# State space loop of a vision tower: the heads' products turned to channels on partitions

## The reference, cut to what matters

```python
z = zxbcdt[..., :D_INNER]                       # D_INNER = 256, the gate
xBC = silu(causal_conv(zxbcdt[..., 256:768], 4 taps) + conv_b)
xs, Bc, Cc = xBC[..., :256], xBC[..., 256:384], xBC[..., 384:]     # xs as 4 heads of 64
h = h * dA_t + (dt_t * x_t) * B_t               # scan over the 36 tokens
y_t = einsum('bhpn,bn->bhp', h, C_t)
y = ys + D_skip * xs
y = y * silu(z)
y = y * rsqrt(mean(y * y, -1) + 1e-05) * gnorm_w
return y @ W_out
```

## Time and profile before

| | |
|---|---|
| median of 3 runs | 1536.03 us (1534.56 to 1537.8) |
| the profiled execution | 1539.4 us |
| its span in the trace | 1537.6 us |
| TensorE matmul busy | 1271.7 us, 83% of the span |
| VectorE busy | 768.6 us, 50% |
| ScalarE busy | 736.6 us, 48% |
| GpSimd busy | 389.9 us, 25% |
| the state space stage | about 490 to 669 us of the span |

### The profile page before, as it was taken

How to read it: one execution, slowest core, us unless ns; L and a number is a source line. 1 busy time by engine, 2 the same in 40 slices (tenths; PEclk the granted TensorE clock), 3 DMA queues, 4 the chain that set the end, 5 groups by cost and what they waited for, 6 DMA issues and landing times. The chain is left out here.

```text
span 1537.6 us, 34523 instructions
## 1 busy us (share of the span) xinstructions
PE 1271.7 (83%) x10636; PEld 1111.1 (72%) x10636; DVE 768.6 (50%) x2481; ACT 736.6 (48%) x2620; POOL 389.9 (25%) x721
## 2 busy tenths in 40 slices
PE   6999579999983899945357599996799889947996
PEld 3777469999972899845357588885799777835885
DVE  0388641111125477734665345555533248863775
ACT  0488434444421455531124167663344248831895
POOL 0156510100001166632347100001101011111452
PEclk9999869999995899968579799998799979976998
DMA  6000010100001000000232100000000100012442
GB/s 235 13 1 0 1 35 15 28 14 14 14 0 42 1 1 0 0 14 1 84 104 49 55 1 0 0 0 1 28 18 17 37 6 1 0 38 65 137 136 66
DMA packets 41923, 48.88 MB, mean 32 GB/s; under 512 B 8085, under 2 KB 31236, under 8 KB 41580
## 3 DMA queue, kind: packets, MB, share of 16 engines
q1 hardware_dynamic: 34876, 36.79, 8.1%
q0 software_dynamic: 4176, 6.56, 1.6%
q10 hardware_dynamic: 2784, 4.47, 0.8%
HBM read 41.78 MB, written 6.56 MB: 31 GB/s over the span
## 5 line engine op out<-in xcount | busy, mean ns | idle before, releaser
L964 ACT ACTIVATE f_hid<-quad_bank,f_b1s 128x512 f32<-128x512 f32 (+1 forms) x240 | 147.9, 645 | 188.0 <-PE quad_bank L895 187.8
L1009 DVE SCALAR_TENSOR_TENSOR f_y<-bank,GATE,f_y 128x128 f32<-128x128 f32 x288 | 81.0, 344 | 253.7 <-PE bank L908 253.5
L908 PEld LDWEIGHTS bank<-f_w2s,f_hid 128*128 128x128 f32 x1728 | 201.7, 192 | 3.7
L908 PE MATMUL bank<-f_w2s,f_hid 128*128 128x128 f32 x1728 | 203.2, 275 | 0.0
L895 PE MATMUL quad_bank<-f_xp,f_w1p 128*128 128x512 f32 (+1 forms) x720 | 168.4, 383 | 16.8 <-DVE f_xp L990 16.8
L459 ACT ACTIVATE a_E<-quad_bank,a_shift 108x108 f32<-108x108 f32 x528 | 177.6, 356 | 4.3 <-DVE a_shift L523 3.9
L895 PEld LDWEIGHTS quad_bank<-f_xp,f_w1p 128*128 128x128 f32 x720 | 125.6, 193 | 37.8 <-issue 17.0
L459 ACT ACTIVATION_READ_ACCUMULATOR a_E<-quad_bank,a_shift 108x1 f32 x528 | 112.7, 213 | 0.0
L299 POOL TENSOR_TENSOR a_ve<-a_mv,const 108x1 f32<-108x1 f32 x66 | 12.5, 190 | 391.8 <-DVE a_mv L578 391.8
L1551 PE MATMUL bank<-ss_xp,ss_wtap 128*128 128x108 f32 x704 | 88.0, 284 | 23.2 <-DVE ss_xp L1631 20.3
L368 PE MATMUL quad_bank<-a_qk 19*108 19x108 f32 (+1 forms) x1056 | 101.3, 275 | 3.4 <-ACT a_E L459 0.6
(11 more groups left out here) (369 smaller groups left out, 2807.1 us busy)
## 6 DMA issues: line engine op xcount, KB each, us to landing
a_wqk<-in_a_wqk SPq DMA_DIRECT2D x24, 256.0 KB
pats<-in_patches SPq DMA_DIRECT2D x3, 1296.0 KB, 18.7
a_wo<-in_a_wo SPq DMA_DIRECT2D x24, 128.0 KB, 2.0
pats<-in_patches ACTq DMA_DIRECT2D x2, 1296.0 KB, 14.3
f_w1s<-in_f_w SPq DMA_DIRECT2D x8, 256.0 KB, 2.7
f_w2s<-in_f_w SPq DMA_DIRECT2D x8, 256.0 KB, 3.0
f_w1a<-in_f_w SPq DMA_DIRECT2D x1, 2048.0 KB, 9.9
f_w2a<-in_f_w SPq DMA_DIRECT2D x1, 2048.0 KB, 14.6
```

The costliest lines, as they stand in the source:

```text
L908: mm = pe.matmul(m.bank[n % 2][0:W, g * D:(g + 1) * D], hid[:, n % 2, c, g * W:(g + 1) * W], w2s[:, u, c * 128:(c + 1) * 128], start=(c == ...
L964: act.activation(hid[:, n % 2, c, 0:k * W], m.quad_bank[:, (n * chunks + c) % 4, 0:k * W], func, bias=b1s[:, u, c:c + 1]).then_inc(hid_rea ...
L1009: ins = dve.scalar_tensor_tensor(out=h, in0=y[:, (g - c0) * D:(g - c0 + 1) * D], scalar=m.GATE[:, bass.ds(e + g * 8, 1)], in1=h, op0=ALU.m ...
```

## The change

The gate's product is turned: the weights are stationary and the input moves, so z comes out with channels on partitions, as two matmuls of 128 channels by 108 tokens. No copy of the input is needed. The heads' products are turned the same way: each head's dt x is stationary (64 columns), its decay matrix moves, and the result lies at PSUM partitions 0 to 63 or 64 to 127, two heads side by side and two one behind the other. `xd` is made from the silu result, which has channels on partitions already, with D as a column. `ys`, `yz`, `zs` are [128, 216]. yz is then the stationary operand of the output projection as it is: its transposes and the copy `yT` are gone. The sum of squares over channels is now a sum over partitions: ScalarE squares yz, and TensorE multiplies the squares (stationary) with a column of ones, two matmuls that accumulate; ScalarE reads that with scale 1/256 and bias epsilon, and GpSimd makes one instruction of rms, in step t for group t-4, behind n1 of t-5. `xd` stands first in GpSimd's step. The D row is not loaded any more. The core of the diff, declarations left out:

```diff
         def _(pool):
+            pool.wait_ge(w_loaded, 64)
+
             def step(t, par):
                 q = 1 - par
-                if live(t, 1):
-                    g = t - 1
-                    at_least(pool, z_psum, g - 1)
-                    pool.tensor_copy(xTs[:, q, :], m.XT[:, bass.ts(g, P)]).then_inc(xts_ready, 1)
+                if live(t, 2):
+                    g = t - 2
+                    pool.wait_ge(silu, g + 1)
+                    at_least(pool, ys_ready, g - 1)
+                    pool.tensor_tensor(xd[:, par, :, :], sx[:, par, 0:2, :], ch[:, 22:24].unsqueeze(2).broadcast_to([128, 2, P]),
+                                       ALU.mult).then_inc(xd_ready, 1)
                 if live(t, 5):
...
-                if live(t, 3):
-                    g = t - 3
+                if live(t, 4):
+                    g = t - 4
                     pool.wait_ge(ssq_ready, g + 1)
-                    pool.tensor_tensor(ssq[:, q, :], ssq[:, q, :], m.inv_cw[0:P, :], ALU.mult).then_inc(rms_steps, 1)
-                    pool.wait_ge(rms_steps, g * 2 + 1)
-                    pool.tensor_tensor(ssq[:, q, :], ssq[:, q, :], m.eps[0:P, :], ALU.add).then_inc(rms_steps, 1)
-                    pool.wait_ge(rms_steps, g * 2 + 2)
                     at_least(pool, sum_ready, g - 1)
-                    pool.tensor_tensor(rms[:, q, :], ssq[:, q, :], m.mhalf[0:P, :], ALU.pow).then_inc(rms_ready, 1)
+                    pool.tensor_tensor(rms[:, par, :], ssq[:, par, :], m.mhalf[0:P, :], ALU.pow).then_inc(rms_ready, 1)
...
-                    pe.wait_ge(xts_ready, g + 1)
                     at_least(pe, z_ready, g)
-                    pe.matmul(m.bank[1][0:P, 0:CW], xTs[:, par, :], win[:, 0:CW], start=True, stop=True).then_inc(z_psum, 1)
-                if live(t, 4):
-                    g = t - 4
-                    pe.wait_ge(yz_ready, g + 1)
-                    at_least(pe, yt_ready, g)
                     for c in range(2):
-                        mm = pe.transpose(m.bank[0][:, c * P:(c + 1) * P], yz[:, par, c * 128:(c + 1) * 128], m.ident[0:P, 0:P])
-                    mm.then_inc(yt_psum, 1)
+                        mm = pe.matmul(m.bank[1][:, c * P:(c + 1) * P], win[:, c * 128:(c + 1) * 128], m.XT[:, bass.ts(g, P)], start=True, stop=True)
+                    mm.then_inc(z_psum, 1)
...
                     for n in range(NS):
-                        cols = slice(n * 64, (n + 1) * 64)
-                        mm = pe.matmul(y_bank[0:P, cols], M[:, q, n, :], xdt[:, q, cols], start=True, stop=True)
+                        mm = pe.matmul(y_bank[n % 2 * 64:(n % 2 + 1) * 64, n // 2 * P:(n // 2 + 1) * P], xdt[:, q, n * 64:(n + 1) * 64], M[:, q, n, :],
+                                       start=True, stop=True)
                     mm.then_inc(y_psum, 1)
+                if live(t, 4):
+                    g = t - 4
+                    pe.wait_ge(sq_ready, g + 1)
+                    at_least(pe, ssq_ready, g)
+                    for c in range(2):
+                        mm = pe.matmul(m.bank[0][0:P, 0:1], sq[:, par, c * P:(c + 1) * P], m.one, start=(c == 0), stop=(c == 1))
+                    mm.then_inc(ssq_psum, 1)
...
-                    pe.wait_ge(yt_ready, g + 1)
+                    pe.wait_ge(yz_ready, g + 1)
                     at_least(pe, sum_ready, g)
                     for c in range(2):
-                        mm = pe.matmul(o_bank[0:P, 0:D], yT[:, c * P:(c + 1) * P], wout[:, c, :], start=(c == 0), stop=(c == 1))
+                        mm = pe.matmul(o_bank[0:P, 0:D], yz[:, par, c * P:(c + 1) * P], wout[:, c, :], start=(c == 0), stop=(c == 1))
...
-                    act.wait_ge(yt_psum, g + 1)
-                    at_least(act, o_psum, g)
-                    act.activation(yT[:, :], m.bank[0][:, 0:2 * P], ACT.Copy).then_inc(yt_ready, 1)
+                    act.wait_ge(ssq_psum, g + 1)
+                    at_least(act, rms_ready, g - 1)
+                    act.activation(ssq[:, par, :], m.bank[0][0:P, 0:1], ACT.Identity, scale=m.inv_cw[0:P, :], bias=m.eps[0:P, :]).then_inc(ssq_ready, 1)
...
-                    act.activation(sq[:, :], yz[:, q, :], ACT.Square, accum_out=ssq[:, q, :]).then_inc(ssq_ready, 1)
+                    act.activation(sq[:, q, :], yz[:, q, :], ACT.Square).then_inc(sq_ready, 1)
...
                     dve.wait_ge(xd_ready, g + 1)
-                    dve.tensor_tensor(ys[:, :], xd[:, q, :], y_bank[0:P, 0:CW], ALU.add).then_inc(ys_ready, 1)
+                    dve.tensor_tensor(ys[:, :], xd[:, q, :, :].rearrange("p c j -> p (c j)"), y_bank[:, 0:2 * P], ALU.add).then_inc(ys_ready, 1)
```

More of the change, by code:

```diff
@@ L1393, in state_space_phase @@
         silu = sem("silu")
-        xts_ready = sem("xts_ready")
         xc_psum = sem("xc_psum")
@@ L1409, in state_space_phase @@
         yz_ready = sem("yz_ready")
+        sq_ready = sem("sq_ready")
+        ssq_psum = sem("ssq_psum")
         ssq_ready = sem("ssq_ready")
-        rms_steps = sem("rms_steps")
         rms_ready = sem("rms_ready")
-        yt_psum = sem("yt_psum")
-        yt_ready = sem("yt_ready")
         o_psum = sem("o_psum")
@@ L1428, in state_space_phase @@
         wtap = sb("wtap", [128, TAPS, 512])
-        drow = sb("drow", [P, NS])
-        xd = sb("xd", [P, 2, CW])
-        ys = sb("ys", [P, CW])
+        xd = sb("xd", [128, 2, 2, P])
+        ys = sb("ys", [128, 2 * P])
         xp = sb("xp", [128, 2, TB, PADDED])
@@ L1435, in state_space_phase @@
         sx = sb("sx", [128, 2, 4, P])
-        xTs = sb("xTs", [128, 2, P])
         cum = sb("cum", [P, 2, NS, P])
@@ L1442, in state_space_phase @@
         xdt = sb("xdt", [P, 2, CW])
-        zs = sb("zs", [P, 2, CW])
-        yz = sb("yz", [P, 2, CW])
-        sq = sb("sq", [P, CW])
+        zs = sb("zs", [128, 2, 2 * P])
+        yz = sb("yz", [128, 2, 2 * P])
+        sq = sb("sq", [128, 2, 2 * P])
         ssq = sb("ssq", [P, 2, 1])
         rms = sb("rms", [P, 2, 1])
-        yT = sb("yT", [128, 2 * P])
         yt = sb("yt", [P, 2, D])
@@ L1460, in _ @@
         def _(sp):
-            for dst, src in ((win, io["ss_win"]), (ch, io["ss_ch"]), (drow, io["ss_drow"])):
+            for dst, src in ((win, io["ss_win"]), (ch, io["ss_ch"])):
                 sp.dma_start(dst[:, :], src).then_inc(w_loaded, 16)
@@ L1509, in _ @@
         def _(pe):
-            pe.wait_ge(w_loaded, 80)
+            pe.wait_ge(w_loaded, 64)
             pe.wait_ge(prepared, 4)
@@ L1581, in step @@
                     at_least(act, mix_ready, g - 1)
-                    at_least(act, xd_ready, g - 1)
                     act.activation(xc[:, par, :], m.bank[3][0:P, 0:CW + P], ACT.Copy).then_inc(xc_ready, 1)
@@ L1585, in step @@
                     at_least(act, yz_ready, g - 1)
-                    act.activation(zs[:, par, :], m.bank[1][0:P, 0:CW], ACT.Tanh, scale=0.5).then_inc(z_tanh, 1)
+                    act.activation(zs[:, par, :], m.bank[1][:, 0:2 * P], ACT.Tanh, scale=0.5).then_inc(z_tanh, 1)
                 if live(t, 4):
                     g = t - 4
-                    act.wait_ge(yt_psum, g + 1)
-                    at_least(act, o_psum, g)
-                    act.activation(yT[:, :], m.bank[0][:, 0:2 * P], ACT.Copy).then_inc(yt_ready, 1)
+                    act.wait_ge(ssq_psum, g + 1)
+                    at_least(act, rms_ready, g - 1)
+                    act.activation(ssq[:, par, :], m.bank[0][0:P, 0:1], ACT.Identity, scale=m.inv_cw[0:P, :], bias=m.eps[0:P, :]).then_inc(ssq_ready, 1)
                 if live(t, 0):
@@ L1603, in step @@
                     act.wait_ge(yz_ready, g + 1)
-                    at_least(act, rms_ready, g - 1)
-                    at_least(act, ssq_ready, g)
-                    act.activation(sq[:, :], yz[:, q, :], ACT.Square, accum_out=ssq[:, q, :]).then_inc(ssq_ready, 1)
+                    at_least(act, ssq_psum, g - 1)
+                    act.activation(sq[:, q, :], yz[:, q, :], ACT.Square).then_inc(sq_ready, 1)
                 if live(t, 6):
@@ L1615, in _ @@
             dve.memset(xp[:, :, :, 0:TAPS - 1].rearrange("p a b k -> p (a b) k"), 0.0).then_inc(prepared, 1)
-            dve.wait_ge(w_loaded, 80)
+            dve.wait_ge(w_loaded, 64)
             dve.tensor_tensor(wtap[:, :, :], wtap[:, :, :], win[:, CW:CW + 512].unsqueeze(1).broadcast_to([128, TAPS, 512]),
@@ L1636, in step @@
                     at_least(dve, xc_psum, g - 1)
+                    at_least(dve, xd_ready, g - 1)
                     dve.scalar_tensor_tensor(out=sx[:, q, :, :].rearrange("p c j -> p (c j)"), in0=th[:, q, :, :].rearrange("p c j -> p (c j)"),
@@ L1653, in step @@
                     dve.wait_ge(z_tanh, g + 1)
-                    dve.scalar_tensor_tensor(out=zs[:, par, :], in0=zs[:, par, :], scalar=1.0, in1=m.bank[1][0:P, 0:CW],
+                    dve.scalar_tensor_tensor(out=zs[:, par, :], in0=zs[:, par, :], scalar=1.0, in1=m.bank[1][:, 0:2 * P],
```

(8 more changed lines are left out.)

## The result

The changed kernel took 1554.91 us (median of 4 runs, 1551.89 to 1560.13) against 1536.91 for the kernel before beside it: ratio 1.0121, 95% interval [1.009, 1.0153]. Slower, as forecast, but by 18.0 us where 4.9 were forecast, and outside the range of 1537 to 1545.5. Its profiled execution took 1554.92 us (span 1553.1, mean granted clock 0.891).

What follows compares the result with a forecast made beforehand. TensorE was taken to bound the kernel at 6.63 us a step, with the VectorE-GpSimd loop about as long after the change. Middle +3.1, end +2.2, start -0.4 gave +4.9 and 1541 us; eight in ten: 1537 to 1545.5.

Steps and rivals of the forecast that it cites:

- TensorE's step: Middle of the state space loop: gate -0.17, heads -0.10, squares +0.36, so 6.72 us a step instead of 6.63.
- Gate and heads: TensorE's step: the gate as four records takes 0.45 us, the heads as four pairs of 64 columns 0.62.
- Rival 1: TensorE: pairs don't overlap or ones products cost more, step 7.0 us, total 1545; chance 0.13.
- Rival 3: Not slower: drains vanish, heads 0.36, TensorE's step 6.46, VectorE-GpSimd loop 6.5 us, total 1535.5; chance 0.15.
- the sum with losses at both ends: Heads on TensorE: 0.09 lost going in, first pair 0.15, two pairs of 0.092, 0.19 going out: 0.61 us.
- The loop: VectorE and GpSimd: normalisation, VectorE's step, n1, rms in a circle, 6.66 and 7.31 us by turns, mean 6.98.
- I take 6.80 for the step: Step length forecast for the middle of the loop, +0.17 us over 18 steps, +3.1 us in all.
- The allowance of 0.2: VectorE-GpSimd loop: 0.2 us allowed for waits for ScalarE that VectorE's part may still hold.
- The bound of 7.0: Upper bound for the step in the middle of the loop: 7.0 us, +0.37 a step, +6.7 us in all.
- Rival 2: VectorE-GpSimd loop: n1 beside VectorE's gate slows both, step 6.9 to 7.0 us, total 1543.3; chance 0.15.
- The end: Last two steps, without convolutions: about 4.4 us each with rms behind n1, +2.2 us (bounds 0 and +3).
- The start: Dropped D row load lets the taps' load issue earlier: -0.4 us, or 0 if the transfer is bound by bytes.

Runs made afterwards that it cites:

- e8: Changed kernel with GpSimd in the order rms, n1, xd and the heads in the order 0, 2, 1, 3: ratio 1.0070 to the kernel before.
- e1: Changed kernel with xd moved behind rms in GpSimd's step, rms still behind n1: ratio 1.0032 to the kernel before.
- e2: Changed kernel with rms moved ahead of the three n1 instructions, xd still first: ratio 1.0024 to the kernel before.
- e3: Changed kernel with GpSimd in the order rms, n1, xd (both moves): ratio 1.0039 to the kernel before.
- e6: Changed kernel run again, unaltered: ratio 1.0100 to the kernel before.
- e4: Kernel before, old layout, with rms worked out one step later, behind n1 and xd: ratio 1.0173 to the kernel before.
- e5: Kernel before with five added passes over H two stages behind the state space loop, as a delay: ratio 1.0043 to the kernel before.
- e7: Changed kernel with GpSimd order rms, n1, xd, and squares and column of ones in bf16: ratio 0.9987 to the kernel before.

## Why the prediction was right or wrong

- **TensorE's step: right.** Forecast 6.72, measured 6.77 where nothing else sets it. Gate and heads 0.54 + 0.52 = 1.06 (forecast 0.45 + 0.62 = 1.07, with the loss on the way in counted to the heads; it shows in the gate's distance). The squares were mis-sized a little: 0.41 against 0.36. Rival 1 (7.0) is out. Rival 3 (heads 0.36) is out too; the sum with losses at both ends was the right one, though my reason for it, pairs on the two halves by turns, was not: e8 has one change of halves in place of three and takes the same time.
- **The loop: right in kind, wrong in size, and this is the step that failed.** I wrote "xd moves to the front of GpSimd's step and waits for silu, made in the step before: nothing waits there." True of the wait, but I priced the moved instruction at its new place at nothing: it now runs beside VectorE's two-input products, inside a loop that my own sum had at 6.66 and 7.31. Measured: +0.35 on L1629 in each step, +0.35 on the mask in every second, 0.50 of the step's 0.64 (e1). The other 0.14 is TensorE's: e1's step is 6.76 and TensorE's part grew by 0.13. Over all steps this is 7.7 us (142.95 against 135.28). That rms in the loop uses up the room was forecast; with rms out of the loop the slow products cost nothing (e2).
- **"I take 6.80 for the step".** The allowance of 0.2 that led from 6.98 to 6.80 was sound for what it covered: without the contention the loop takes 6.50 and 7.04 (e1), where the sum said 6.66 and 7.31. VectorE's part was put too long, 3.7 and 4.2, where e1 has 3.56 and 3.97. The bound of 7.0 was not a bound: it held nothing for a resource that two engines share. 18 x 0.17 = 3.1 became 18 x 0.61 = 10.9, of which 1.3 are the 18th spacing, where the end begins.
- **Rival 2** had the family right (GpSimd and VectorE slow each other in the loop) and the place wrong: the n1 instructions still take 0.45 to 0.47, and VectorE's product with the gate beside them (L1658) 0.45 and 0.53 by turns, as L1669 did before (0.45 and 0.54). From L1648 to the last n1 it is now 593.26 - 591.65 = 1.61 in one step and 1.68 in the other, against the 1.66 and 1.81 on which I built it. (Its sum gives 1543.2, not 1543.3.)
- **The end: right.** 4.4 a step forecast, 4.44 measured; +2.2 forecast, 8.88 - 6.59 = +2.3 measured. It is rms behind n1: e1, where only xd moved, keeps it (20.1 for the last four spacings), e2 and e3 don't have it (15.3 and 14.6).
- **The start: wrong, small.** The taps' load was issued 1.33 behind the stage's first instead of 1.74, but the product that needs it began 7.17 behind it instead of 7.24, and 7.95 in e6. The 0.4 saved at the issue did not arrive at the product; two executions of the old layout have 7.13 and 7.74 there (e4, e5), so 0.4 is below what these profiles can tell. That the transfer is bound by its bytes, my other bound, is not shown.
- **Carried to the total.** The stage gives 13.5 of the 15.8 by which e6's median lies above before, and 13.5 alone is more than the 9.5 at which my range ended. The other 2.3 us stay open; of the first result's 18.0 they are 4.5, or 8.6 by that execution's own stage (+9.4). Outside the stage ten profiled executions vary from 1355.9 to 1362.3 (the delay of e5 taken off); in the first of the changed kernel this went with the granted clock of the attentions. Chance is one reading of it. It is not the only one: with the new layout the median exceeds that of before by more than the stage does in all but e1 (e2 5.8 against 1.6, e3 4.1 against 0.3, e7 -1.8 against -7.8, e8 9.9 against 0.6; e1 5.3 against 5.4), so a cost of some us outside the stage, or in starts that were not profiled, is not ruled out. My range took the kernel's scatter from three runs of before that lay within 3.2 us, where 29 lay within 21: the 0.2% that I took for what a measurement can tell was too small a figure.

The Trainium skill has the contention that I missed (SBUF — State Buffer, Who interferes with whom, and for the lock SBUF: two separate sides): a VectorE instruction with two SBUF inputs contends with a GpSimd instruction that reads SBUF, and whichever starts first holds the shared ports for its whole length. The trace agrees with the first half: L1629 at 0.95 instead of 0.60 beside xd, and 0.60 in e1 and e3, where xd runs elsewhere. The second half does not fit by the recorded starts: at 589.11 L1629 started 0.46 ahead of xd and still took 0.95, the same as at 592.30 in e2, where xd had started first. GpSimd's rstd (L1493, 588.69 to 589.60) was under way then too, but e1 has the same pair without xd, and L1629 took 0.60:

```profile
578.86 0.91 POOL L1493 TENSOR_TENSOR ss_rstd<-ss_ve,const 108x1 f32<-108x1 f32 x1
579.28 0.60 DVE L1629 TENSOR_TENSOR ss_cum<-const,DTA 108x432 f32<-108x432 f32 x1
```

There the measurement decides, as far as GpSimd's recorded start can be trusted to 0.46 us.

## What to carry to other kernels

When an instruction is moved, price it at its new place: which instructions of the other engine with two inputs in SBUF it will run beside, and whether these stand in the loop that sets the pace. When the sum of a loop comes out near the bound of the other engine, there is no room left in it: a term put at nothing then counts in full, so price each. And when two causes only cost together in the middle, as here, moving either out of the way repairs it (one block in e1 or in e2); moving rms, as in e2, repairs the end as well. A new order is best tried alone in the old layout first, as e4 does.

## What the runs showed of the hardware

- GpSimd's product of 128x216 beside VectorE's product of 108x432 (both inputs in SBUF): 0.95 instead of 0.60 for VectorE, and for GpSimd 0.79 to 0.89 instead of 0.55 when it also runs beside VectorE's instruction ahead of or behind that product (e2 has 0.55 where the two start within 0.06 of each other). In the step shown, VectorE's two and xd fill 589.11 to 590.59, 1.48 us; alone they take 0.60 + 0.27 + 0.55 = 1.42. They come near to running one after the other.
- The heads' eight records of 64 weight columns and 108 moving ones take 0.52 to 0.53 in either order of the two halves, where eight of 108 weight columns and 64 moving ones took 0.72.
- A product with one moving column takes 0.10 a record in f32 (four in 0.41), and 0.06 in bf16, which also needs half the records (two in 0.12).
- The start of the stage differs by 4.0 us between two executions of the changed kernel (41.03 and 45.02): its first two convolutions took 5.35 and 3.79 in one, 6.94 and 5.42 in the other, and the product that needs the taps' load began 0.8 later.
